# A mixture of attention experts: the value-bias rows of an expert pair on a semaphore of their own, loaded earlier

## The reference, cut to what matters

```python
def _expert(x, Wqkv, bqkv, Wo, bo, g1, be1, W1, bf1, W2, bf2, g2, be2):
    b, s, d = x.shape
    qkv = x @ Wqkv.T + bqkv
    q, k, v = jnp.split(qkv, 3, axis=-1)
    ...
    attn = jax.nn.softmax(jnp.einsum('bhqd,bhkd->bhqk', q * scale, k), axis=-1)
    ctx = jnp.einsum('bhqk,bhkd->bhqd', attn, v).transpose(0, 2, 1, 3).reshape(b, s, d)
    ctx = ctx @ Wo.T + bo
    x = _layernorm(x + ctx, g1, be1)
    h = jax.nn.gelu(x @ W1.T + bf1, approximate=False)
    h = jax.nn.gelu(h @ W2.T + bf2, approximate=False)
    return _layernorm(x + h, g2, be2)
...
_, idx = jax.lax.top_k(probs, K)
...
return jnp.einsum('ebsd,bse->bsd', eo, gated)
```

## Time and profile before

| what | value |
|---|---|
| median of 3 runs | 448.14 us (447.12 to 450.26) |
| profiled execution | span 449.3 us from first to last instruction, 7597 instructions; no other time of it is given |
| PE busy | 412.4 us, 92% of the span |
| DVE busy | 214.4 us, 48% |
| ACT busy | 120.0 us, 27% |
| chain that ended last | PE 64%, DVE 15%, issue 7%, DMA 6%, ACT 3% |
| transfers | 104.57 MB, mean 233 GB/s over the span |

### The profile page before, as it was taken

How to read it: one execution, slowest core, us unless ns; L and a number is a source line. 1 busy time by engine, 2 the same in 40 slices (tenths; PEclk the granted TensorE clock), 3 DMA queues, 4 the chain that set the end, 5 groups by cost and what they waited for, 6 DMA issues and landing times.

```text
span 449.3 us, 7597 instructions
## 1 busy us (share of the span) xinstructions
PE 412.4 (92%) x2819; PEld 308.1 (69%) x2819; DVE 214.4 (48%) x631; ACT 120.0 (27%) x347; POOL 35.0 (8%) x68
## 2 busy tenths in 40 slices
PE   7998999994748989999998999999999999999996
PEld 6698655883247878797784668756778896394492
DVE  6744464457994254462754527557442631111102
ACT  2322313303220102251531325442111332222121
POOL 4000010011232001001000010002010000000000
PEclk9999999998699999999999899999999999999999
DMA  8999579222002200899999999336300299999900
GB/s 274 402 422 338 223 292 388 93 95 93 0 2 91 97 0 3 338 395 423 418 295 304 355 423 288 90 117 274 131 0 0 85 427 421 419 422 421 415 12 24
DMA packets 19631, 104.57 MB, mean 233 GB/s; under 512 B 3550, under 2 KB 5470, under 8 KB 7946
## 3 DMA queue, kind: packets, MB, share of 16 engines
q1 hardware_dynamic: 19306, 104.07, 60.9%
q10 hardware_dynamic: 288, 0.02, 0.0%
HBM read 103.82 MB, written 0.26 MB: 232 GB/s over the span
## 4 chain that ended last, share of the span: by engine, by line
PE 64%; DVE 15%; issue 7%; DMA 6%; ACT 3%; POOL 2%; DVEq 1%; SPq 1%; POOLq 0%; ACTq 0%
PE ps L1108 12%; PE ps L1096 8%; PE ps L1770 6%; PE ps L1510 5%; DMA dense<-in_l_w 5%; PE ps L1490 3%; PE ps L1499 3%; PE ps L1593 2%; PE ps L1084 2%; PE ps L1252 2%; PE ps L1092 1%; DMA ew<-in_l_wq 1%; PE ps L1185 1%; PE ps L1835 1%; PE ps L1289 1%
## 5 line engine op out<-in xcount | busy, mean ns | idle before, releaser
L1084 PE MATMUL ps<-ident 128*128 128x128 f32 x372 | 48.4, 284 | 2.7 <-POOL ident L647 2.7
L1084 PEld LDWEIGHTS ps<-ident 128*128 128x128 f32 x372 | 46.0, 199 | 5.1 <-POOL ident L647 2.7
L1108 PEld LDWEIGHTS ps<-y_t,ew 128*128 128x128 f32 x352 | 39.9, 192 | 1.7 <-issue 1.7
L1108 PE MATMUL ps<-y_t,ew 128*128 128x128 f32 x352 | 40.2, 275 | 0.0
L1096 PE MATMUL ps<-ew,y_t 128*128 128x512 f32 x72 | 32.7, 597 | 0.0
L1510 PE MATMUL ps<-y_t,ew 128*128 128x128 f32 x224 | 27.5, 277 | 0.0
L1510 PEld LDWEIGHTS ps<-y_t,ew 128*128 128x128 f32 x224 | 26.1, 192 | 0.8 <-issue 0.7
L768 ACT ACTIVATE prob_store<-ps,nmax_s 128x128 f32<-128x128 f32 x56 | 19.7, 384 | 14.6 <-DVE nmax_s L1957 14.6
L1096 PEld LDWEIGHTS ps<-ew,y_t 128*128 128x128 f32 x72 | 13.0, 190 | 13.5 <-issue 13.3
L758 ACT COPY y_t<-ps 128x256 f32<-128x256 f32 x16 | 5.7, 373 | 61.5 <-PE ps L1092 61.1
L2561 DVE SCALAR_TENSOR_TENSOR t<-prob_store 128x512 f32<-128x512 f32 x6 | 4.2, 692 | 36.4 <-ACT prob_store L1018 20.4
(11 more groups left out here) (514 smaller groups left out, 751.0 us busy)
## 6 DMA issues: line engine op xcount, KB each, us to landing
ew<-in_l_w SPq DMA_DIRECT2D x20, 1024.0 KB, 21.8
dense<-in_l_w SPq DMA_DIRECT2D x12, 1024.0 KB, 21.2
ew<-in_l_wv SPq DMA_DIRECT2D x8, 1024.0 KB, 13.8
ew<-in_l_wk SPq DMA_DIRECT2D x7, 1024.0 KB, 16.3
ew<-in_l_wq SPq DMA_DIRECT2D x6, 1024.0 KB, 12.0
erows<-in_l_rows SPq DMA_DIRECT2D x4, 1280.0 KB, 12.5
ew<-in_l_wo SPq DMA_DIRECT2D x5, 1024.0 KB, 14.8
ew<-in_gqa_wq SPq DMA_DIRECT2D x3, 1024.0 KB, 10.9
```

Of the source, the lines that this page charges most:

```text
L1084: pe.matmul(ps[:, b, 3 * P:4 * P], ident[:], ident[:], start=True, stop=True)
L1108: last = pe.matmul(ps[:, b, m * n:(m + 1) * n], w[:, c, (first + m) * P:(first + m + 1) * P], in_t[:, c, 0:n], start=(c == 0), stop=(c == ...
```

## The change

The two BV transfers of a pair leave load_pair_rows and become a function of their own, load_pair_value_rows, with a semaphore of their own, l2_value_rows_landed. For the first pair (experts 2 and 3) SP now waits for l2_v_ready and issues them right after the output weights of experts 2 and 3, ahead of the query weights of experts 5 and 6; the other four row transfers stay where they were, after l2_expert_added. For the second pair (experts 5 and 6) the two BV transfers go first of the six, between the two waits, which change places. v_bias of a pair waits only for the BV rows. The other rows are awaited at the start of the pair's first_norm; their counts on l2_rows_landed0 fall from 112 and 208 to 80 and 144, since the BV transfers no longer count there.

```diff
+            def load_pair_value_rows(experts):
+                for a, e in enumerate(experts):
+                    sp.dma_start(erows[:, a, BV, :], A["l2_rows"][e][BV:BV + 1].broadcast_to([P, D])) \
+                        .then_inc(sig("l2_value_rows_landed"), 16)
+
             def load_pair_rows(experts):
                 for a, e in enumerate(experts):
                     r = token_half[a]
-                    sp.dma_start(erows[:, a, BV, :], A["l2_rows"][e][BV:BV + 1].broadcast_to([P, D])) \
-                        .then_inc(sig("l2_rows_landed0"), 16)
...
             load_l2("o", 3, e3)
+            sp.wait_ge(*at("l2_v_ready", 2))
+            load_pair_value_rows((e2, e3))
             sp.wait_ge(*at("l2_k_projected", 4))
             load_l2("q", 5, e5)
             sp.wait_ge(*at("l2_v_projected", 2))
             load_l2("q", 6, e6)
             sp.wait_ge(*at("l2_expert_added", 1))
-            sp.wait_ge(*at("l2_v_ready", 2))
             load_pair_rows((e2, e3))
...
             load_l2_small(e4, 1)
+            sp.wait_ge(*at("l2_v_ready", 5))
+            load_pair_value_rows((e5, e6))
             sp.wait_ge(*at("l2_expert_added", 3))
-            sp.wait_ge(*at("l2_v_ready", 5))
             load_pair_rows((e5, e6))
...
-            rows_landed = {0: 16, 1: 16, 2: 112, 3: 32, 4: 208, 5: 48}
+            rows_landed = {0: 16, 1: 16, 2: 80, 3: 32, 4: 144, 5: 48}
 
             def v_bias(t):
-                dve.wait_ge(*at(f"l2_rows_landed{t % 2}", rows_landed[t]))
+                if t in L2_PAIRS:
+                    dve.wait_ge(*at("l2_value_rows_landed", 32 * (L2_PAIRS[t] + 1)))
+                else:
+                    dve.wait_ge(*at(f"l2_rows_landed{t % 2}", rows_landed[t]))
...
                 settle()
-                if t not in L2_PAIRS:
+                if t in L2_PAIRS:
+                    dve.wait_ge(*at("l2_rows_landed0", rows_landed[t]))
+                else:
                     dve.wait_ge(*at("l2_residual_ready", t + 1 - sum(k < t for k in L2_PAIRS)))
```

## The result

The changed kernel takes 447.5 us (median of 20 runs, 446.49 to 449.56). The kernel before, run 20 times beside it, takes 450.22 us (447.12 to 452.98). The ratio is 0.9938 with an interval of 0.9922 to 0.9954: 2.7 us by the medians, 0.6%, and within the 1% that had the largest chance. The predicted 444.4 us is 3.1 us too low and 447.5 us lies above the range of 442.9 to 446.9 us.

The account below looks back on a forecast made before the run. Bound: a mostly TensorE chain, with a 20.52 us row transfer delaying the first pair's value addition and a slow clock behind the gap. 2.11 + 0.50 + 1.17 = 3.78 us off 448.14 gave 444.4 us, range 442.9 to 446.9 us.

Parts of the forecast that it names:

- The wait of the first value addition: First expert pair, VectorE: with its own semaphore the addition can start at 238.27 us, no longer waiting for all six rows.
- the start of the weighted sum: First pair, TensorE line 1577: starts 1.09 us after the scores, at 242.49 and not 244.60 us; gain 2.11 us.
- the two clock terms: Behind the gap, at full clock: gathering matmuls save 0.50 us, first half of the output projection 1.17 us.
- the value rows: First pair's queue: issued from about 219.5 us, landing at 227 to 229 us, before VectorE is ready; cost nothing.
- the query weights: Queued behind the value rows, issued about 7 us later; landing 229.6 to 243.2 us, needed at 253.2 us; cost nothing.
- the small matrices: Dense step's loads behind the last output weights: use moves to 280.2 us, margin about 2.7 us, no cost.
- the norm released by TensorE: Pair's first layer norm, now awaiting the four other rows: TensorE still releases it, margin 3.7 us, cost nothing.
- the late value rows: Rival at the first pair's additions: value rows still land too late, so no gain, 448.1 us; chance 0.10 (no effect).
- the dry queue: Rival: SP held 6.25 us at the value semaphore starves the queue, 449.7 us; chance 0.06 with other such surprises.
- taken off the median: 444.4 us: Final step: the 3.78 us gain subtracted from the 448.14 us median, the profiled span being 449.3 us.
- I take 1.67 us: Slow clock behind the first pair's gap: its whole loss, 1.67 us, goes with the gap; bounds 0 to 1.70 us.
- the gap goes, the clock's loss stays or was never in the timed runs: Rival at the first pair: only the 2.11 us of idleness is gained, giving 446.0 us; chance 0.14.

Follow-up runs that it names:

- run 20: No label of a run: the kernel before was run 20 times beside the changed kernel; 450.22 us (447.12 to 452.98).
- the 0.96 us above: TensorE's gap in the profile of the kernel before with 22 instead of 3 identity matmuls in the retrieval sublayer; 448.62 us, ratio 0.9953.
- VectorE's own gap: Changed kernel with three additions on VectorE between the first pair's two value additions, so TensorE waits without a transfer; 450.96 us, ratio 1.0034 to the kernel before.
- the filled wait in the retrieval sublayer: 22 instead of 3 identity matmuls before the fifth head: on the changed kernel 446.63 us (0.9957) and 448.18 us (0.9961), on the kernel before 448.62 us (0.9953).
- the third profile of the kernel before: Profile from the second follow-up timing of the kernel before, unchanged; 450.02 us against 450.31 us, ratio 0.9997.

## Why the prediction was wrong

**What held.** The wait of the first value addition, the start of the weighted sum (1.09 us behind the scores, as the second pair showed), the two clock terms, the value rows, the query weights and the small matrices at no cost, the norm released by TensorE: each stands in the profile after as its step said. The value rows and the last of the other rows even landed earlier than forecast (226 and 241.6 us, not 227 to 229 and 243.2 us). The rivals of the late value rows and of the dry queue are refuted by these landings and by the missing wait at 279.69 us.

**The first step that failed: "taken off the median: 444.4 us".** The gain was read from an execution with a span of 449.3 us and taken off a median of three runs, 448.14 us. The step "1.2 us below that span, inside their spread" compared a span with a time: the 1.75 us around the span belong on top, so the profile stood for about 451.0 us, 2.9 us above that median. Twenty runs put the median of before at 450.22 us, and 448.14 us was 2.1 us low. Of the miss of 3.1 us, 2.1 us come from here. Off the execution that it was read from, the same gain gives 451.0 - 3.8 = 447.2 us, 0.3 us from the measured 447.5 us, but that nearness is partly luck: that execution was about 0.8 us above the median of before, and the gain was about 1.1 us too large for the median.

**The second: "I take 1.67 us", one profile's full loss for every execution.** The 3.78 us are right for the profiled execution and too much for the median, which gained 2.7 us; this is the rest of the miss, about 1 us. Span and mean clock are known for 136 comparable executions of the kernel before and 32 of the changed one. The mean spans are 448.4 and 445.9 us, 2.5 us apart. The time lost to the clock is 9.4 us on average before and 8.6 us after: 0.8 us, with a standard error of 0.3 us, and not 1.67 us. That is an average in which about half of the executions of before pay for the fall, if falls elsewhere are equally frequent in both. The rest, 2.5 - 0.8 = 1.7 us, is idleness, against 2.11 us in the sum.

These averages mix chips. In the one set that has both kernels on one chip (34 and 12 executions) the clock's part is 0.1 us with a standard error of 0.5 us, and the rest 2.0 us with one of 0.4 us. So the clock gave back less than 1.67 us in both, but how much less is not settled. Among executions with the mean clock of 0.985, spans of before run from 445.0 to 448.1 us (22 of them, median 447.0), those of the changed kernel only from 444.7 to 445.6 us (10, median 445.15): at one clock, 1.85 us. The three quickest of before (445.0 to 445.1 us) lie among those of the changed kernel, which fits a gap that is sometimes small, such as the 0.96 us above.

**The rival "the gap goes, the clock's loss stays or was never in the timed runs"** was right in part: no fall is left without the gap, but not every gap brings one (at this place it is in three of the four profiles with a gap above 1 us, VectorE's own gap among them, and in none of the other ten). The gain of 2.7 us lies between its price, 2.11 us, and the forecast's, 3.78 us. It was given 0.14 as if it were all or nothing; the averages show a mixture.

The Trainium skill (TensorE: Matmul & The Clock Gate, Part 1) says that the activity window runs freely, so that one kernel measures different numbers of slow matmuls from run to run; the pair of profiles of one kernel, with a fall behind 2.04 us of idleness and none behind 1.84 us, agrees that the same code need not meet the same clock.

**What stays open.** Why the row transfers ended about 1 us earlier in one execution, and 1.4 us earlier with the new order; and in how many single executions the fall behind the gap occurs, since each has only a mean clock. A lower bound of those without it can be estimated: every profile without the filled wait in the retrieval sublayer loses about 6.8 us or more to the clock between 108 and 139 us, which alone makes a mean clock of 0.985, so the 22 of 136 executions of before at that clock have nothing left for a fall at the pair.

## What to carry to other kernels

A gain that is read from one profile belongs to that execution: take it off that execution's own time (span plus what lies around it), and ask how often the timed executions share the loss. Where a consumer counts several transfers on one semaphore, it waits for the last, so give what is needed first its own count; here that alone was enough, and so, nearly, was moving it ahead in the queue. When an idle engine is followed by a lower clock, price the two apart, the idleness by the wait and the clock by how many executions show it.

## What was not expected of the hardware

- Issue order changed when a group of transfers ended, with the same bytes behind the same weights: the last row landed at 241.8 us and not at 243.2 us once two of the six went ahead of two matrices of 1 MB, and 17.0 to 18.1 us after its issue in all six profiles with that order, not 19.4 to 20.7 us as in the eight without.
- The granted clock behind a similar idle stretch differs between executions of one program. At the pair it fell to 1.2 GHz behind gaps of 2.04 and 1.99 us and stayed at 2.4 GHz behind one of 1.84 us; in other kernels it fell behind 1.89 us, and stayed behind 0.57, 0.94 and 0.96 us.
- The length of the gap doesn't decide alone. Before the fall at 350 us in the third profile of the kernel before, the only idle stretches of TensorE from 340 us on are of 0.47 and 0.46 us; the changed kernel has the same two at 344.44 and 345.78 us, and no fall behind them.
- Falls of about 3.4 us, each worth 1.7 us by the granted clock, come at other places too. Between 108 and 139 us every profile without the filled wait has four or five times that, in part while TensorE waits anyway; near 34, 174 and 352 us they come in some executions and not in others. By their mean clocks this sum runs from 6.7 to 10.7 us over the 32 executions of the changed kernel, a spread larger than what this change is worth.
